# Channel attention on one core: pointwise product and residual as one product, centre taps on ScalarE, group statistics in two parts

## The reference

```python
x = x + _L0_conv_ref(_gn(x), w_qkv, w_dw, w_proj, temperature)
x = _L1_conv_ref(x, pw_w, ..., dwk_w, ..., dw1_w, ...)
...
# _gn: group norm, 32 groups of 3 channels, per image
# _L0_conv_ref: 1x1 conv to q, k, v; depthwise 3x3 conv; l2-normed q, k;
#               8 heads of channel attention (12x12 scores); 1x1 projection
# _L1_conv_ref:
x_pw = bn(einsum(x, pw_w)) + x
out = bn(dwconv13(x_pw)) + bn(x_pw * dw1_w)
return gelu(out)
```

## Time and profile before

| | us |
|---|---|
| median of 3 runs | 917.54 |
| lowest, highest of them | 916.73, 1200.09 |
| the profiled execution's own time | 916.39 |
| its span, first to last instruction | 914.7 |
| channel attention within it (first instruction to last stored image) | about 0 to 163.8 |
| large convolution | about 164 to 260 |
| the rest (transformer) | up to 914.7 |

### The profile page before, as it was taken

How to read it: one execution, slowest core, us unless ns; L and a number is a source line. 1 busy time by engine, 2 the same in 40 slices (tenths; PEclk the granted TensorE clock), 3 DMA queues, 4 the chain that set the end, 5 groups by cost and what they waited for, 6 DMA issues and landing times.

```text
span 914.7 us, 17153 instructions
## 1 busy us (share of the span) xinstructions
PE 798.1 (87%) x6224; PEld 668.8 (73%) x6224; DVE 600.0 (66%) x1716; ACT 459.7 (50%) x761; POOL 363.8 (40%) x428
## 2 busy tenths in 40 slices
PE   1799997699832769999999999999999999999997
PEld 1577774598821547878888788878888888888775
DVE  4899996665432467677767776676667667657431
ACT  1155554210320325665666666656566566666653
POOL 3211112730041344454544644546446456444421
PEclk9999997699955688999999999999999999999999
DMA  4630000010003321302303023033032231330000
GB/s 87 94 56 0 0 0 1 5 26 12 1 3 75 78 56 24 78 21 59 77 4 78 28 52 79 10 70 67 13 79 57 40 79 36 61 80 10 10 9 9
DMA packets 28999, 37.19 MB, mean 41 GB/s; under 512 B 10696, under 2 KB 25856, under 8 KB 28928
## 3 DMA queue, kind: packets, MB, share of 16 engines
q1 hardware_dynamic: 28928, 36.24, 19.0%
HBM read 25.06 MB, written 11.17 MB: 40 GB/s over the span
## 4 chain that ended last, share of the span: by engine, by line
PE 58%; DVE 8%; issue 2%; ACT 2%; POOL 1%; DMA 1%; SPq 1%; DVEq 0%; ACTq 0%; POOLq 0%
PE ps L1144 19%; PE ps L1133 13%; PE ps L1085 4%; PE ps L1069 4%; PE ps L1054 3%; PE ps L1098 3%; PE ps L1071 2%; PE ps L1059 2%; DVE tr_mf L1394 2%; PE ps L1123 2%; PE ps L1103 1%; PE ps L1158 1%; PE ps L1111 1%; DVE tr_xT L1376 1%; PE ps L1048 1%
## 5 line engine op out<-in xcount | busy, mean ns | idle before, releaser
L1144 PE MATMUL ps<-w,tr_hid 128*128 128x96 f32 x1536 | 189.6, 275 | 4.4 <-DVE tok L1487 4.4
L1144 PEld LDWEIGHTS ps<-w,tr_hid 128*128 128x128 f32 x1536 | 184.5, 192 | 9.5 <-issue 5.4
L1303 ACT ACTIVATE tr_hid<-ps,b 128x512 f32<-128x512 f32 x192 | 130.9, 687 | 108.1 <-PE ps L1133 106.4
L989 POOL TENSOR_SCALAR_AFFINE_SELECT tr_pT<-tr_pT 128x768 f32<-128x768 f32 x64 | 55.3, 865 | 191.4 <-ACT tr_pT L1287 190.5
L1394 DVE TENSOR_REDUCE tr_mf<-ps 128x4 f32<-128x1024 f32 (+2 forms) x96 | 101.0, 1084 | 42.9 <-PE ps L1071 42.3
L1287 ACT ACTIVATE tr_pT<-ps 128x1024 f32<-128x1024 f32 (+1 forms) x96 | 86.4, 918 | 59.9 <-PE ps L1085 59.8
L1487 DVE SCALAR_TENSOR_TENSOR tok<-ps,tr_gate,tok 128x96 f32<-128x96 f32 x224 | 55.5, 310 | 65.5 <-PE ps L1144 59.1
L605 DVE SCALAR_TENSOR_TENSOR ca_qk<-ps,dw,ca_qk 96x225 f32<-96x225 f32 (+1 forms) x256 | 97.7, 447 | 0.0
L1069 PE MATMUL ps<-keys,tr_qs 96*128 96x256 bf16 (+1 forms) x384 | 73.6, 270 | 21.5 <-DMA keys<-parts 14.2
L1133 PE MATMUL ps<-tr_xh,tr_wh 96*128 96x512 f32 x192 | 86.8, 452 | 5.5 <-DVE tr_xT L1376 3.8
L1133 PE MATMUL ps<-tr_xh,tr_wl 96*128 96x512 f32 x192 | 75.9, 395 | 0.0
(11 more groups left out here) (233 smaller groups left out, 1695.3 us busy)
## 6 DMA issues: line engine op xcount, KB each, us to landing
parts<-tr_part SPq DMA_DIRECT2D x96, 96.0 KB
tr_qs<-parts SPq DMA_DIRECT2D x16, 288.0 KB, 4.2
keys<-parts SPq DMA_DIRECT2D x16, 288.0 KB, 5.3
tr_qs<-parts SPq DMA_DIRECT2D x16, 192.0 KB, 5.7
keys<-parts SPq DMA_DIRECT2D x16, 192.0 KB, 6.2
w<-in_L_ffn_w SPq DMA_DIRECT2D x4, 576.0 KB
chan<-in_x SPq DMA_DIRECT2D x4, 384.0 KB, 5.1
windows<-lines_d SPq DMA_DIRECT2D x96, 13.0 KB, 1.6
```

Source lines behind the costliest of these rows:

```text
L989: pool.affine_select(out=block, in_=block, compare_op=ALU.is_ge if causal(n // 2) else ALU.not_equal, fill=0.0, base=0, pattern=[[0, H], [ ...
L1144: ins = nc.tensor.matmul(ps[:, RES, C * t:C * (t + 1)], hid[:, e % 2, c, P * t:P * (t + 1)], m.ffn[j // PAIRS].w2[:, e * HC + c, :], start ...
L1303: nc.scalar.activation(hid[:, e % 2, c, :], ps[:, H0 + step % 2, :], ACT.Gelu, bias=m.ffn[j // PAIRS].b1[:, step:step + 1]).then_inc(s_h, 1)
```

## The change

- `pointwise` and `keep_result` go. `result` now multiplies the image itself by the matrix (identity + pw), and adds attention times a projection into which the same matrix has been multiplied once in the setup (`later_weights`). The bias is added by ACT in `keep_pointwise`, which reads PSUM with a per-partition bias. In `result` the small product comes ahead of the product with the image.
- The centre taps of q and k go from DVE to ACT (`centre_taps`, two activations with a per-partition scale), so a DVE step begins with tap 1 and waits for `s_ctr`.
- Group statistics are taken of images 0 to 3 first, and of images 4 to 15 after the first weights are kept.
- Folding of batch norms and later weights moves between steps 0 and 1 (`fold_weights` on DVE, `later_weights` on PE), that of the 13x13 lines between steps 1 and 2 (`fold_lines`). ACT waits for the second part's numbers after step 1.
- On POOL the clearing of the windows moves behind step 1. On SP the last weights' loads move ahead of the store of the lines.

```diff
+GN_PARTS = ((0, 4), (4, 16))
...
+        def steps(eng, step, after_first=None, after_second=None):
             step(0, 0, 0, 2)
+            if after_first:
+                after_first()
             step(1, 1, 1, 2)
+            if after_second:
+                after_second()
             with eng.Fori(1, B // 2 - 1) as j:
...
+                def group_rstd(k):
+                    lo, hi = GN_PARTS[k]
+                    pool.wait_ge(s_gdve, 5 * k + 5)
+                    link(pool.tensor_scalar(gm[:, 3, lo:hi], gm[:, 3, lo:hi], 1e-5, 0.0, ALU.add, ALU.add))
+                    pool.tensor_tensor(gm[:, 1, lo:hi], gm[:, 3, lo:hi], m.power[0:C, 0:hi - lo], ALU.pow).then_inc(s_grs, 1)
...
+                def clear_windows():
+                    pool.wait_ge(s_rn, 3)
+                    pool.memset(m.win[:, :, :, :], 0.0).then_inc(s_zero, 1)
+                    pool.wait_ge(s_zero, 1)
...
                 def result(c, slot):
-                    pe.wait_ge(s_ptk, c + 1)
-                    nc.tensor.matmul(ps[0:C, 7, 0:N], m.ident[0:C, 0:C], m.x[:, bass.ds(c, 1), :].rearrange("p b n -> p (b n)"),
-                                     start=True, stop=False)
                     pe.wait_ge(s_at, c + 1)
                     pe.wait_ge(s_aps, c + 1)
                     nc.tensor.matmul(ps[0:C, 6, 0:C], at[:, 1, :], m.wT[0:C, M_PROJ0, :], start=True, stop=True).then_inc(s_ap, 1)
+                    pe.wait_ge(s_ptk, c + 1)
+                    nc.tensor.matmul(ps[0:C, 7, 0:N], m.wT[0:C, M_PW, :], m.x[:, bass.ds(c, 1), :].rearrange("p b n -> p (b n)"),
+                                     start=True, stop=False)
                     pe.wait_ge(s_aps, c + 2)
...
-                def pointwise(c):
-                    pe.wait_ge(s_x1, c + 2)
-                    nc.tensor.matmul(ps[0:C, 7, 0:N], m.wT[:, M_PW, :], x1[:, :], start=True, stop=True).then_inc(s_pt, 1)
...
+                def later_weights():
+                    pe.wait_ge(s_vec, 16 * n_vec)
+                    nc.tensor.transpose(ps[0:C, 5, 0:NV], m.vecrows[:, :], m.ident[0:NV, 0:NV]).then_inc(s_vecT, 1)
...
+                    group_means(1, 0)
+                    group_means(1, 1)
+                    pe.wait_ge(s_fold, 1)
+                    turn_weights(M_PW, 5, 5)
+                    pe.wait_ge(s_wT, 6)
+                    pe.wait_ge(s_shift, 2)
+                    nc.tensor.matmul(ps[0:C, 6, 0:C], m.raw[:, M_PROJ0, 0:C], m.wT[0:C, M_PW, :],
+                                     start=True, stop=True).then_inc(s_wp, 1)
+                    pe.wait_ge(s_wp, 2)
...
+                def centre_taps(b, slot):
+                    act.wait_ge(s_qk, b + 1)
+                    for t in range(2):
+                        nc.scalar.activation(qkc[:, slot, t, :], ps[0:C, slot, N * t:N * (t + 1)], ACT.Copy,
+                                             scale=m.dw0[:, t, CENTRE:CENTRE + 1]).then_inc(s_ctr, 1)
...
+                def keep_pointwise(c):
+                    act.wait_ge(s_out, c + 2)
+                    nc.scalar.activation(m.pw[:, :].rearrange("c (x b y) -> c b y x", b=B, y=HH)[:, bass.ds(c, 1), :, :],
+                                         ps[0:C, 7, 0:N].rearrange("c (b y x) -> c b y x", b=1, x=WW), ACT.Identity,
+                                         bias=m.pwb[:, :]).then_inc(s_ptk, 1)
...
+                image_stats(0, 4, 0)
+                group_variance(0)
...
+                keep_variance(0)
...
+                keep_weights(0, 0, 2, 2)
+                keep_weights(1, 2, 5, 3)
+                group_shift(0)
+                keep_weights(2, 7, 4, 4)
+                image_stats(4, B, 8)
...
                 def step(b, slot, back, ahead):
                     c = b - 1
-                    dve.wait_ge(s_qk, b + 1)
-                    convolve(b, slot, 0, 7)
+                    dve.wait_ge(s_ctr, 2 * b + 2)
+                    convolve(b, slot, 1, 7)
...
-                steps(dve, step)
+                steps(dve, step, fold_weights, fold_lines)
```

More of the change, by code:

```diff
@@ L114, in buffers @@
     m.bn = sb("bn", [C, 2, 3])
+    m.pwb = sb("pointwise_bias", [C, 1])
     m.wT = sb("wT", [C + 1, NM, C])
@@ L173, in channel_attention @@
     s_lines, s_bias = sem("lines_stored"), sem("conv_bias")
-    s_ones, s_pt, s_ptk = (sem(n) for n in ("ones_row", "pointwise", "pointwise_kept"))
+    s_ptk, s_wp, s_ctr = sem("pointwise_kept"), sem("projection_folded"), sem("centre_taps")
     s_win = [sem(f"windows{k}") for k in range(SLOTS)]
@@ L177, in channel_attention @@
     s_tap = [sem(f"ca_tap{t}") for t in range(2)]
[L178 removed]
+    (s_xn, s_qk, s_v, s_vc, s_ss, s_rn, s_kn, s_T, s_trs, s_sc, s_mx, s_nm, s_ex, s_rc, s_at, s_ap, s_aps, s_out) = (
         sem(f"ca_{n}") for n in ("normed", "qk", "v", "v_kept", "squares", "norms", "k_scaled", "turned", "turned_kept",
[L180 removed]
+                                 "scores", "max", "shift", "exp", "recip", "attn", "attnproj", "attnproj_kept", "out"))
     n_vec = len(VECTORS) + 2
@@ L321, in _ @@
             def _(pe):
-                for s in (s_T, s_sc, s_ap, s_out, s_pt):
+                for s in (s_T, s_sc, s_ap, s_out):
                     pe.sem_inc(s, 1)
@@ L377, in step @@
                         turn(c, other)
-                    if back == 2:
-                        pointwise(c - 1)
                     if ahead:
@@ L493, in step @@
                     if back == 2:
-                        keep_result(c - 1)
+                        keep_pointwise(c - 1)
                     if back:
                         scale_k(c, other)
-                    if back:
                         keep_turned(c)
+                    if ahead:
+                        centre_taps(b + 1, other)
                     if ahead == 2:
@@ L511, in _ @@
                 normed(1, 1)
-                steps(act, step)
+                centre_taps(0, 0)
+                steps(act, step, after_second=wait_second_part)
                 squares(B - 1, 1)
-                keep_result(B - 2)
+                keep_pointwise(B - 2)
                 scale_k(B - 1, 1)
                 keep_turned(B - 1)
-                keep_pointwise(B - 2)
                 exponential(B - 1, 1)
                 keep_product(B - 1)
-                keep_result(B - 1)
                 keep_pointwise(B - 1)
@@ new lines, in group_variance @@
+                def group_variance(k):
+                    lo, hi = GN_PARTS[k]
+                    group = Link(dve, s_gdve, 5 * k + 1)
+                    dve.wait_ge(s_gm, 2 * k + 1)
+                    group(nc.vector.tensor_scalar(gm[:, 2, lo:hi], ps[0:C, 6, lo:hi], 1.0 / GN_CH, None, ALU.mult))
+                    group(nc.vector.tensor_tensor(gm[:, 3, lo:hi], gm[:, 0, lo:hi], gm[:, 2, lo:hi], ALU.subtract))
+                    link(nc.vector.tensor_tensor(gm[:, 1, lo:hi], gm[:, 3, lo:hi], gm[:, 3, lo:hi], ALU.mult))
+                    group(nc.vector.tensor_tensor(gm[:, 3, lo:hi], gm[:, 1, lo:hi], mv[:, lo:hi, 1], ALU.add))
@@ new lines, in keep_variance, with group_shift @@
+                def keep_variance(k):
+                    lo, hi = GN_PARTS[k]
+                    dve.wait_ge(s_gm, 2 * k + 2)
+                    nc.vector.tensor_scalar(gm[:, 3, lo:hi], ps[0:C, 7, lo:hi], 1.0 / GN_CH, None, ALU.mult).then_inc(s_gdve, 1)
+                def group_shift(k):
+                    lo, hi = GN_PARTS[k]
+                    dve.wait_ge(s_grs, k + 1)
+                    nc.vector.scalar_tensor_tensor(shift[:, lo:hi], gm[:, 2, lo:hi], -1.0, gm[:, 1, lo:hi],
+                                                   ALU.mult, ALU.mult).then_inc(s_shift, 1)
@@ L551, in _, with keep_weights @@
-                for n, (first, count, bank) in enumerate(((0, 5, 2), (5, 5, 3), (10, 2, 4))):
+                keep_variance(0)
+                def keep_weights(n, first, count, bank):
                     dve.wait_ge(s_wps, n + 1)
@@ new lines, in fold_lines @@
+                def fold_lines():
+                    dve.wait_ge(s_dwk, 16)
+                    link(nc.vector.tensor_scalar(m.dwk[:, :], m.dwk[:, :], m.bn[:, 0, 1:2], None, ALU.mult))
+                    centre = R * KW + R
+                    link(nc.vector.scalar_tensor_tensor(m.dwk[:, centre:centre + 1], m.vec[:, V_DW1:V_DW1 + 1], m.bn[:, 0, 2:3],
+                                                        m.dwk[:, centre:centre + 1], ALU.mult, ALU.add))
+                    link(nc.vector.memset(m.lines[:, :], 0.0))
+                    nc.vector.tensor_copy(m.lines[:, LEAD * KW:(LEAD + KW) * KW].rearrange("c (k j) -> c k j", j=KW),
+                                          m.dwk[:, :].rearrange("c (j k) -> c k j", k=KW)).then_inc(s_fold, 1)
+                    nc.vector.tensor_tensor(m.bn[:, 1, 1:2], m.bn[:, 1, 1:2], m.bn[:, 1, 2:3], ALU.add).then_inc(s_fold, 1)
```

173 lines of the change are left out of this document (72 added, 101 removed).

## The result

The changed kernel takes 909.34 us (median of four runs, 907.71 to 909.79) where the kernel before took 917.24 beside it on the same chip (median of four, 916.73 at best). One of the four executions of the kernel before took 1200.09 us and is left out of the ratio, which is 0.9912, with a 95% interval of 0.99 to 0.9924: 7.9 us less between the medians. The forecast was 909.5. The profiled execution took 909.01, its span 907.3 where 914.7 stood before and 907.1 was forecast.

What follows compares the result with a forecast made beforehand. The prediction took DVE's work and a chain through all engines as level bounds of the loop, the change relieving one. Setup 4.6 + loop 1.8 + tail 1.2 = 7.6 us gained, giving a median of 909.5, range 901 to 916.

Steps and rivals of the forecast that it cites:

- The chain: Loop through all engines once a step, attention matrix to maximum and back: 7.43 and 7.52 us, mean 7.47, the whole step.
- The loop: Thirteen steps between maximum in steps 2 and 15: 0.14 us less each, 1.8 us gained, between -1.1 and 10.1.
- the 0.26: One loop step of two: small product kept 0.11 us sooner, maximum 0.15 sooner after the kept transposes.
- rival 5: Centre taps' move does nothing: with them on DVE the time would be the same within 1.8 us; no chance given.
- The setup: Work up to maximum(1): it comes at about 48.0 us, where it was at 52.60; gain 4.6, between 2.2 and 8.2.
- the mis-sized term: Setup, L619's scaling on DVE beside POOL's power: expected to end with the power, bounds 0 and 2.3 us, taken 1.2.
- the rule's second half: Setup: a DVE operation with two SBUF inputs also waits for GpSimd reading SBUF; L614 would wait, about 0.8 us more.
- The tail: Behind the last product: copy and pointwise product go, 1.62 us; about 0.3 and 0.09 come back; gain 1.2.
- 1 (DVE-bound): Loop: DVE is the bound, the chain has unseen slack; steps of 6.69 us, time 901; chance 0.10.
- 2 (short fold, clock kept): Setup: the fold is short and PE's clock stays high; maximum(1) at 44.4, time 906; chance 0.15.
- 3 (ACT-bound): Loop: ACT becomes the bound with taps of 0.59 us, 0.3 a step, and a fold of 2.4 more; 916; chance 0.15.
- 4: Loop: PE's clock falls to 0.50 after waits of about 0.5 us; 67 us more, about 976; chance 0.03.

Runs made afterwards that it cites:

- the best kernels: Changed kernel with k's square and norm first and one value tap behind the query-key product: 904.52 us; the same with the fold ahead of step 0: 903.36 us.
- the last variant of the loop: Changed kernel with k's norms first, the value's third tap behind the query-key product, and the weights folded ahead of step 0: 903.36 us, ratio 0.9842.

## Why the prediction was right

The time was right (909.5 for 909.34), and so was what bounds the loop. That it was right to 0.2 us is luck: the three terms came to 9.36 us where 7.6 was forecast, 1.4 of it in the setup, and an effect behind channel attention that it didn't foresee took 2 us away again.

**Which bound.** The chain, not DVE. Four things show it: the waits of 0.76 and 0.42 ahead of `maximum` (forecast: 0.4 to 0.7), one more DVE operation a step at no cost, the taps' move alone worth nothing in the kernel before, and steps 0.43 shorter where the way to the transposes was shortened and DVE's work was not.

**The loop, 1.8 us forecast, 2.06 measured.** The step was to be 7.33 and is 7.31. The halves, too: 0.26 was to go from the step of 7.43 and 0.02 from the one of 7.52, in which ACT sits 0.26 in "issue". That makes 7.17 and 7.50; measured are 7.15 and 7.47. Both reasons given for the 0.26 are in the rows: the small product is kept 0.50 after the matrix's end (92.59 for 92.09), and `maximum` starts 1.20 after the kept transposes (97.64 for 96.44), each as forecast. ACT's taps were put at 0.44 and 0.36 from start to start; they are 0.47 and 0.37. What moving the small product is worth by itself was not tried.

**That the centre taps' move does nothing in the end, within 1.8 us (rival 5),** was wrong. Undone, it costs 4.3, some 2.6 without the experiment's own bubble. The step that failed is the one that took the two bounds apart: it held the loop at the chain's 7.33 with the taps on DVE. They were level, at 7.43 to 7.47 each, as the prediction itself had written a paragraph earlier, and a level bound that isn't relieved keeps the loop where it is. Without the move the chain's 0.14 can't be had either.

**The setup, 4.6 forecast, 5.98 measured.** First shift 11.5 and 11.56, image 0's taps to 23.6 and 23.12, PE's value taps to 24.1 and 23.9. The terms from 24.1 to the power's end add up to 29.2, where the prediction writes 29.7; the power ended at 29.59. Then the mis-sized term: L619 was "taken 1.2" beside POOL's power, and is 0. With it done at 27.76, the five transposes ran beside the power instead of behind it, and step 1 began at 31.39 for 32.6. The low clock there was as forecast: queries, keys and four value taps took 5.0 us (31.39 to 36.36). `maximum(0)` is 1.26 earlier than forecast (38.44 for 39.7) and `maximum(1)` 1.38 (46.62 for 48.0); the way between the two was right, 8.3 and 8.18. The Trainium skill, page "SBUF — State Buffer", section "Who interferes with whom", has such an operation held until the one on GpSimd ends. This case shows that for the clearing (2.91, and 0.27 once it was moved) and not for the power: 0.27 from 27.49, when the power had 2.1 us to go. L614 doesn't test the rule's second half: it began at 26.77, ahead of POOL's operation of 26.83, and was done before the power began, so the 0.8 that the prediction would have added for it had nothing to wait for. Where the rule and the measurement differ, on L619, the measurement decides; the clearing and the power differ in a way that the rule doesn't name.

What the setup's gain consists of was not asked in the prediction. The clearing's move alone is 2.6 of it in M1, and the prediction looked only at what it would meet where it went, not at what it would free where it left, though the row of 2.91 stood in the text. The first part's smallness is worth 5.85 in M1, in the profiled execution of the split of 12 and 4 (3.7 in the medians). That is 8.4 together for 5.98; what costs the difference was not tried.

**The tail, 1.2 forecast, 1.32 measured**, by the rows; no run tried its terms one by one.

**What was not foreseen: 2 us given back.** The span is 7.4 shorter for 9.36. The packing of the convolution starts at 166.40 where it started at 174.41: of 9.36, 8.0 is left. 1.0 of the 1.4 went in the 24 transposes, at 355 ns instead of 275, and 0.4 in the 32 ahead of them (5.35 us for 4.96), with a clock of 0.52 in the ten microseconds behind the last store, where it was 0.76 before. In the profiled execution with one more DVE operation a step the loss is absent and the span is 905.9, so it is not tied to the change's code. But that the change makes it more frequent is not excluded: the transposes are slow in six of the eleven profiled executions of the changed kernel and its variants, and in none of the three of the kernel before and its variants. About 0.6 more is lost by 347 us; from 267 to 347 the clock is 0.64, and 0.68 in the same code before. That was not tried by itself.

**Rivals.** 1 (DVE-bound) falls by the extra operation, but is what bounds one step of two in the best kernels. 2 (short fold, clock kept) half came true: the fold was short, but the clock was low at step 1 (four products in 2.02 us for the warm 1.03). 3 (ACT-bound) falls: taps of 0.47, not 0.59, though nothing of ACT's margin is left. 4 falls by the clock of 1.00; a low clock showed for one step in the last variant of the loop, behind a wait of 1.31. 5 falls as told.

## What to carry to other kernels

Where an engine's own work and a loop through all engines come to the same step, a part of a change that relieves only one of them is worth nothing alone, and its removal costs all that the loop gained: price them together, and name what is level behind. Look in a trace for an operation that takes ten times what the same shape takes elsewhere (2.91 against 0.27), and for what another engine does until it ends; moving that gave 3.0 us alone. Where TensorE's clock rises at another moment from run to run, compare steps of a loop rather than sums.

## What the runs showed of the hardware that was not expected

- A `tensor_scalar` of DVE in SBUF (96x96) took 2.91 us beside a clearing on POOL and ended with it; beside a power on POOL that lasted 2.29 us it took 0.27. Beside the same clearing, a `scalar_tensor_tensor` of DVE with two inputs in SBUF (L570, 96x96, at 24.03) took 0.32; with the clearing moved it took 0.31.
- The same work begun at the same time (157.67 and 157.69) came to the packing 1.77 us apart, with a granted clock of 0.81 and 0.52 over the ten microseconds. PE had stood 2.83 and 4.20 us before it, but after 1.20 us both outcomes were seen. What decides it was not found.
- In the setup of three executions of the same code the clock rose at other times (1.00, 1.00 and 0.76 from 40 to 44 us), and M1 differed by 1.2 us.
- The clock fell to 0.50 within the loop, for some 3 us, behind a stretch in which PE was busy 2.69 of 4 us and stood for 1.31 us in one piece. In the earlier trace rows too the fall followed more than 1 us without any work of PE. In the changed kernel's loop, where PE is busy 19.30 of 20 us, it stayed at 1.00.
